# Six weight buffers in place of three in the expert feed-forward of a four-layer transformer kernel

## The reference

```python
z = layernorm(x)                                 # 4096 tokens x 128
e = argmax(z @ gate_w.T + gate_b)                # one of 8 experts for each token
h = relu(z @ w1[e].T + b1[e])                    # 128 -> 512
x = x + h @ w2[e].T + b2[e]                      # 512 -> 128
```

## Time and profile before

| | |
|---|---|
| median of 3 runs | 2493.4 us (2490.78 to 2494.09) |
| profiled execution, its own time | 2489.93 us |
| profiled execution, span from first to last instruction | 2488.3 us |
| mean granted TensorE clock | 0.981 |
| TensorE busy | 2321.6 us, 93% of the span |
| VectorE, ScalarE, GpSimd busy | 65%, 60%, 64% of the span |
| transferred | 83.84 MB, mean 34 GB/s |

### The profile page before, as it was taken

How to read it: one execution, slowest core, us unless ns; L and a number is a source line. 1 busy time by engine, 2 the same in 40 slices (tenths; PEclk the granted TensorE clock), 3 DMA queues, 4 the chain that set the end, 5 groups by cost and what they waited for, 6 DMA issues and landing times. The chain is left out here.

```text
span 2488.3 us, 60369 instructions
## 1 busy us (share of the span) xinstructions
PE 2321.6 (93%) x23146; PEld 1789.9 (72%) x23209; DVE 1620.9 (65%) x4106; ACT 1480.6 (60%) x2973; POOL 1588.5 (64%) x2537
## 2 busy tenths in 40 slices
PE   6999999999998999988999999999999968699997
PEld 5778878878876556656777787777778757566665
DVE  5666666666674578874454577777777732478786
ACT  5666666666664478874444466666666523377775
POOL 6788888888885364443333277777777732366664
PEclk9999999999999989999999999999999989899999
DMA  8950000000000010001000000000000036100000
GB/s 284 331 170 2 2 2 2 2 2 2 2 2 1 1 47 2 2 2 33 1 1 1 3 4 4 6 6 4 6 6 4 6 99 182 58 11 10 8 4 35
DMA packets 22911, 83.84 MB, mean 34 GB/s; under 512 B 3969, under 2 KB 10754, under 8 KB 21474
## 3 DMA queue, kind: packets, MB, share of 16 engines
q1 hardware_dynamic: 19474, 72.76, 9.0%
q0 software_dynamic: 3152, 7.21, 0.9%
HBM read 72.75 MB, written 46.79 MB: 48 GB/s over the span
## 5 line engine op out<-in xcount | busy, mean ns | idle before, releaser
L982 POOL TENSOR_TENSOR XR<-XR,T 128x256 f32<-128x256 f32 x504 | 368.4, 731 | 37.7 <-DVE T L861 8.0
L725 ACT ACTIVATE P<-ps 128x384 f32<-128x384 f32 (+1 forms) x512 | 250.5, 542 | 194.8 <-PE ps L2761 191.5
L2761 PE MATMUL ps<-P,V 128*64 128x256 f32 (+3 forms) x4096 | 334.3, 348 | 0.8 <-ACT P L725 0.7
L1529 DVE TENSOR_REDUCE bm<-ps 128x3 f32<-128x384 f32 x512 | 260.3, 550 | 52.4 <-PE ps L2761 49.7
L2761 PEld LDWEIGHTS ps<-P,V 128*64 128x64 f32 (+1 forms) x4096 | 185.9, 123 | 123.1 <-issue 46.3
L1469 ACT ACTIVATE P<-ps 128x768 f32<-128x768 f32 x256 | 207.5, 811 | 76.3 <-PE ps L2761 71.0
L892 DVE TENSOR_REDUCE sm<-ps 128x2 f32<-128x512 f32 (+1 forms) x256 | 129.8, 548 | 168.5 <-PE ps L2761 168.5
L1636 POOL TENSOR_SCALAR_AFFINE_SELECT P<-P 128x512 f32<-128x512 f32 x256 | 165.4, 647 | 103.1 <-ACT P L1469 101.5
L995 POOL TENSOR_TENSOR PS<-P 128x256 f32<-128x256 f32 x256 | 181.3, 732 | 69.1 <-ACT P L725 68.8
L1016 POOL TENSOR_TENSOR ss<-ss,nhalf 128x16 f32<-128x16 f32 x64 | 187.7, 2932 | 5.3
L2761 PE MATMUL ps<-mk,identb 128*128 128x256 bf16 (+1 forms) x768 | 174.8, 296 | 15.2 <-DVE bm L1529 9.0
(11 more groups left out here) (315 smaller groups left out, 6792.8 us busy)
## 6 DMA issues: line engine op xcount, KB each, us to landing
rows_i<-in_zero SPq DMA_DIRECT2D x16, 1208.0 KB, 30.9
rows_o<-in_zero SPq DMA_DIRECT2D x16, 1208.0 KB, 80.5
w<-in_m_w SPq DMA_DIRECT2D x23, 578.0 KB, 4.0
zt<-rows_i SPq DMA_DIRECT2D x23, 128.0 KB, 3.1
rows_o<-yo POOLq DMA_DIRECT2D x23, 128.0 KB, 3.8
stg<-in_t_w SPq DMA_DIRECT2D x11, 256.0 KB, 2.8
XR<-in_x SPq DMA_DIRECT2D x4, 512.0 KB, 9.2
out<-XR SPq DMA_DIRECT2D x8, 256.0 KB, 2.0
```

The source lines that it names most:

```text
L725: e.activation(self.P[at % 6][:, :], K.ps.ap("st", s, g, h)[:, 0:self.w], ACT.Exp, bias=0.0, scale=1.0 if kind == 0 else 0.125).then_inc(K ...
L982: p = po.e.tensor_tensor(x, x, self.T[g % 2][:, par, pr], ALU.add)
L1529: e.tensor_reduce(bm[:, h, :], K.ps.ap("mx", s, g, h)[:, 0:384].rearrange("p (a c) -> p a c", c=128), X, ALU.max, negate=True).then_inc(K. ...
L2761: return self.te.matmul(o, l, r, start=start, stop=True, skip_group_check=True)
```

## The change

There are six buffers `w` and six semaphores `w_in` in place of three, and the buffer of tile j is `j % 6`. SP's load of the weights of tile j waits for the output of tile j-6 in place of tile j-3; the first six loads wait for no output. Everything else in the order of each engine is as before.

```diff
@@ class Moe
+    NW = 6
+
     def __init__(self, K, s):
...
-        self.w = [sb(f"w{s}_{i}", [128, 1156], F32) for i in range(3)]
+        self.w = [sb(f"w{s}_{i}", [128, 1156], F32) for i in range(self.NW)]
...
-        self.w_in = [K.sem(f"wi{s}_{i}") for i in range(3)]
+        self.w_in = [K.sem(f"wi{s}_{i}") for i in range(self.NW)]
...
@@ pe_hidden
-            pe.wait_ge(self.w_in[j % 3], 16 * (j // 3 + 1))
+            pe.wait_ge(self.w_in[j % self.NW], 16 * (j // self.NW + 1))
...
-                p = K.acc(ps[:, 256 * i:256 * i + 256], self.w[j % 3][:, 128 * c:128 * c + 128], self.zT[j % 2][:, :],
+                p = K.acc(ps[:, 256 * i:256 * i + 256], self.w[j % self.NW][:, 128 * c:128 * c + 128], self.zT[j % 2][:, :],
...
@@ sp
-            if j >= 3:
-                sp.wait_ge(*K.ps.read("o", s, j - 3))
-            e.dma_start(self.w[j % 3][:, :], K.t["m_w"][bass.ds(x, 1), :, :].rearrange("a p c -> p (a c)")).then_inc(
-                self.w_in[j % 3], 16)
+            if j >= self.NW:
+                sp.wait_ge(*K.ps.read("o", s, j - self.NW))
+            e.dma_start(self.w[j % self.NW][:, :], K.t["m_w"][bass.ds(x, 1), :, :].rearrange("a p c -> p (a c)")).then_inc(
+                self.w_in[j % self.NW], 16)
```

More of the change, by code:

```diff
@@ L2340, in pe_out @@
                 p = K.acc(ps[:, 128 * i:128 * i + 128], self.h[j % 2][:, c, 128 * i:128 * i + 128],
-                          self.w[j % 3][:, 512 + 128 * c:640 + 128 * c], start=c == 0 and i == 0)
+                          self.w[j % self.NW][:, 512 + 128 * c:640 + 128 * c], start=c == 0 and i == 0)
         p.then_inc(K.ps.full_of("o", self.s, j), 1)
@@ L2362, in act @@
                     ac.wait_ge(*K.ps.filled("o", s, j - 2))
-                ac.wait_ge(self.w_in[j % 3], 16 * (j // 3 + 1))
+                ac.wait_ge(self.w_in[j % self.NW], 16 * (j // self.NW + 1))
                 ac.wait_ge(*K.ps.filled("h", s, j, n))
@@ L2367, in act @@
                     p = e.activation(self.h[j % 2][:, c, :], K.ps.ap("h", s, j, n)[:, 256 * i:256 * i + 256], ACT.Relu,
-                                     bias=self.w[j % 3][:, 1024 + c:1025 + c], scale=1.0)
+                                     bias=self.w[j % self.NW][:, 1024 + c:1025 + c], scale=1.0)
                 p.then_inc(K.ps.out_of("h", s, j, n), 1)
@@ L2444, in dve_out @@
             dv.wait_ge(K.stored_rows[j % 3], 16 * (j // 3))
-        dv.wait_ge(self.w_in[j % 3], 16 * (j // 3 + 1))
+        dv.wait_ge(self.w_in[j % self.NW], 16 * (j // self.NW + 1))
         dv.wait_ge(*K.ps.filled("o", s, j))
         dv.e.tensor_tensor(self.yo[j % 3][:, :, :], K.ps.ap("o", s, j)[:, 0:256].rearrange("p (t c) -> p t c", t=2),
-                           self.w[j % 3][:, 1028:1156].unsqueeze(1).to_broadcast([128, 2, 128]), ALU.add).then_inc(
+                           self.w[j % self.NW][:, 1028:1156].unsqueeze(1).to_broadcast([128, 2, 128]), ALU.add).then_inc(
             K.ps.out_of("o", s, j), 1)
```

## The result

The changed kernel takes 2480.08 us (median of 5 runs, 2476.73 to 2483.42) against 2494.09 of the kernel before in the same comparison (5 runs, 2490.78 to 2496.95). The ratio is 0.9951, with a 95% interval of 0.994 to 0.9963: by this ratio 12.2 us faster, 9.2 to 15.0. The two medians alone are 14.0 us apart, inside that interval. The prediction had 11.8 us, 2481.6 in 2478 to 2487.

What follows compares the result with a forecast made beforehand. TensorE, idling for late loads of `w`, was taken to pace the expert stage. Removed waits gave 11.8 us and the other terms 0, so 2493.4 - 11.8 = 2481.6 us, range 2478 to 2487.

Steps and rivals of the forecast that it cites:

- What bounds the stage: Expert stage's row-tile loop: TensorE paces it, with gaps from late loads of `w`; bare period 3.73 us.
- The wait removed: Loads of `w` in the loop: every wait from tile 3 on goes, 14.1 us of lead, gain 11.8 us.
- The restart of 0.24 us at each wait: TensorE at each wait for `w`: 0.16 us of output-layer drain and 0.08 of slower hidden layer, counted 10 times.
- The first tiles: Start of the loop: loads 3 to 5 go out early, load 1 is issued before them; nothing lost or gained.
- The DMA engines, cost 0: Same bytes per tile need 2.8 us of all engines, 74% of the new period; loads fit, cost 0.
- The stall that stays: Before tile 13, VectorE's `dve_mix` delays the copy of `zT`; stall and low clock unchanged, bounds 2.0 us either way.
- B: At tile 13 the lock or the low clock is missed: 1.6 to 3.6 us more gain, 2478 to 2480; chance 0.04.
- C: Loads in flight together each land later, period between 3.73 and 4.4 us; 2486.5 us at 4.0; chance 0.06.
- D: No change: a second wait, on `zt` or GpSimd's store, ends just behind the removed one; 2491 to 2494; chance 0.05.
- E: Slower: TensorE's clock stays low for 39 us more in the stage after; 2498 us; chance 0.03.
- Two sums in it: Gain by periods in the loop, 12.3 less 0.33 given as 11.9; cases outside the range, given as about 0.12.

Runs made afterwards that it cites:

- the padded one: Kernel before, three buffers and the old wait, with three unused tiles of the same size laid behind them; ratio 0.9996.
- the cut load: Kernel before, three buffers, each load cut in two: hidden layer's weights wait for the hidden layer of tile j-3, the rest for its output; ratio 0.9965.
- the mix in four parts: Changed kernel with the four parts of dve_mix after tiles 14 to 17, not all after tile 10: 2476.36 us; with three buffers, against the kernel before, 0.9996.

## Why the prediction was right

*What bounds the stage: right.* TensorE paced it with gaps, and its bare period is 3.73 us; in the changed kernel it is 3.73 us at every tile but the stall and `pe_bias`.

*The wait removed: right in cause and size.* 11 waits went to none; load 6 has the lead forecast (0.86 us after the hidden layer of tile 2); the stretch fell by 11.78 us against a sum of 11.8. The run with six buffers and the old wait shows the cause, the padded one excludes addresses, and the one with four excludes that depth beyond one more load was needed. In the timed runs it is 12.2, 11.7 and 11.0 us for six, six again and four. That the two sums meet to 0.02 us is luck: with the low clock longer or missing behind the stall, the same subtraction gives 10.6 us for the repeat and 13.5 for four buffers. What doesn't move is the 12.2 us outside the two periods around the stall.

*The restart of 0.24 us at each wait: right to half a microsecond.* The idle time of the waits that count is 9.35 us, with the restarts 11.75, and 12.19 went. The missing 0.4 is in starts a little late that no row marks, such as the 1.88 us from 2070.22 to 2072.10 in place of 1.79. Of the 12.19, 0.47 were lost again at the stall and 0.06 were won at the end, which gives the 11.78.

*The first tiles, nothing: not contradicted, though the profile seems to speak against it.* The 1.8 us lost there lie within what this stretch varies by, with the clock and with the landing of the first rows.

*The DMA engines, cost 0: right, by a poor argument.* The 74% forecast was 77% in the trace, but the step took this share for a capacity; twice the weights went through in the same period.

*The stall that stays: right*, 3.09 us, a tenth above the 2.7 to 3.0 forecast, with the 2.33 us inside it as before. The two periods around it took 12.51 us for 12.04. That the low clock behind it stays was likely but not certain: it came in 6 of the 7 profiles with a stall of 2.7 us or more, missing in the one with four buffers. It came in neither of the two with a stall of under 2 us, nor with the cut load, where the stall was broken in two.

*The rivals.* B, more by the other end of the stall, is half seen: the clock did hold once, with four buffers, and made the stretch 1.7 us shorter; the memsets caught VectorE in every kernel in which neither they nor the mix were moved. C, loads late in part, didn't come with twice the weights either, where one wait of 0.82 us for rows was all. D, no change, had the right suspect, and the prediction dismissed it with a wrong reason: `zt` doesn't keep 14 us of lead. In the kernel before, the rows of tile 4 were issued at 2039.55 and transposed at 2043.40, 3.85 us later; in the changed kernel the rows of tile 6 were issued at 2034.79 and transposed at 2048.70, 13.9 us later. The change itself made this lead, because both transfers stand in one queue and the wait ahead of the rows is the one that was relaxed. Had it not, `zt` would have been next, as the cut load shows with three buffers. E, the clock in the stage after: 349.4 us from gather to end against 349.6, no sign of it; but this part takes 349.4 to 354.4 us in the 13 profiles, so that one pair of them can't exclude a microsecond or two, and the three ratios near 0.995 speak more strongly.

*Two sums in it are slightly off.* 12.29 less 0.33 is 11.96 and not 11.9, and what the range leaves out adds up to 0.11 and not 0.12. Neither changes the forecast.

## What to carry to other kernels

Measure the lead of a load, from the release of its buffer to its first use, and compare it with issue to landing; here the smallest step that made the first larger gave everything, one more buffer, or a cut of the load so that each part is released by its own last reader, with the rows issued ahead of its second wait. In a queue that issues in order, a wait holds back every transfer behind it, so look what else stands there before a wait is moved. After a stall is gone, look at the next one in the same stretch: it may be worth too little to tell before, as the mix in four parts was with three buffers (1.0 us, -1.2 to 3.2), and 4.7 us after. And compare profiles by periods that lie outside a gap whose clock varies, here 18 of 20.

## What the runs showed of the hardware

The 16 DMA engines carried 388 GB/s at a busy share of 1.03, and 175 GB/s at 0.57: the share is no measure of how many more bytes fit. Beside a store's issue and two GpSimd memsets of 0.97 us each, one VectorE TENSOR_SCALAR of 128x128 took 2.33 us, and with the memsets moved away 0.43, where its twin takes 0.29; VectorE's order passed this on to TensorE. After the same idle gap of 3.1 us TensorE's next eight matmuls took 2.00, 3.40, 3.46 or 3.78 us in different executions, at granted clocks of 1.00, 0.55, 0.56 and 0.50, so one profile of a stage with such a gap is uncertain by some 2.7 us, more than half of the 4.7 us that the mix in four parts gained.
